# Second feed-forward stage: masks ahead of a store in the queue, another order at its head, and a last tile finished in four blocks of 128 rows

## The chip, the core and the metric

The kernel is one program on one core of a Trainium2 chip. TensorE (PE), VectorE (DVE), ScalarE (ACT) and GpSimd (POOL) compute; SyncE (SP) issues most of the transfers, POOL some of them. Each engine works through its own list of instructions in order and waits on semaphores that the others raise. The metric is the device time of one execution in microseconds (us); the time given is the median of several executions.

## The reference

A macaron block on x of shape (2, 4096, 256), float32: half a feed-forward stage, attention, half a feed-forward stage.

```
x = x + 0.5 * ffn(layernorm(x))
x = x + attention(layernorm(x))
x = x + 0.5 * ffn(layernorm(x))

ffn(x):
    x_mixed = mix_kernel[0] * x[s-1] + mix_kernel[1] * x[s] + mix_kernel[2] * x[s+1]
    h       = x_mixed @ W1[p] + b1[p]             for nine experts p, 64 wide
    paths   = h @ W2[p] + b2[p]
    scores  = tanh(x_mixed @ Wo1 + bo1) @ Wo2 + bo2
    out     = paths[argmax(scores)]               one expert for each row
    return layernorm(x + out) * gamma + beta
```

The attention takes the absolute value of causal scores, a softmax over them, and its values. The expert's choice is a one-hot row, which the kernel multiplies onto the hidden values of all nine experts.

## The kernel before

**Tiles.** The 8192 rows are 16 tiles of 512 rows; a tile lies as 4 blocks of 128 rows beside each other. `ffn(0)` is the first feed-forward stage, `attention(0)` and `attention(1)` follow, and `ffn(1)` is the second stage. The order on every engine is written out by hand. Each stage has a head, in which tiles 0 to 2 are brought under way, and then the turns t = 0 to 16. In one turn the engines work on several tiles at once: the output product of tile t, the hidden values of tile t+1, the choice of tile t+2, the mixed rows of t+3 and the normalisation of t+5.

**The choice and its masks.** ACT takes tanh (`scores`, L1412), PE multiplies with Wo2 (`route`, L1853), and DVE finds the highest of nine scores in five small steps (`choose`, L929 to L942). PE transposes the one-hot rows (`choice`, L1862), ACT writes them out as `oh_t` (`one_hot`, L1424), and SP's `spread` stores `oh_t` to `oh_scratch` (L467), waits until it has landed, and loads it back three times, spread over the partitions as the mask of five chunks (L472, L474, L476).

**The hidden values.** For each of five chunks c PE forms `hidden(t, c)`, six 512-column matmuls (part of L1756), and DVE adds the bias and multiplies with the mask: `masked(t, 0)` is L956 (both inputs from SBUF), the others are L959 (one input from PSUM). ACT rounds pairs of chunks to float16 (`masked_high`, L1432) and DVE takes what is left over (`masked_low`, L965). PE's `path(t, c)` multiplies them with W2, for chunks 0 to 3 in 12 matmuls of 256 columns, three for each block of rows, and for chunk 4 in float32 (L1882, four matmuls, recorded as eight). Within a chunk it goes over the four blocks, so all four are complete only behind the last matmul of the tile.

**The mixed rows.** `mixed_before` (L818) and `mixed_behind` (L826) on DVE add the two neighbours onto what ACT has begun (`middle`, L1377). ACT's `x_high` (L1385) and DVE's `mixed_low` (L833) split the sum into two float16 parts; `hidden(t, 0)` waits for the second. ACT's `normalised` is L1363 and `transposed` L1369; PE's `transposed` is L1764.

**The end of a tile.** `result` (L913, DVE) adds the product onto the tile's rows. ACT squares and sums them (`squares`, L1393), POOL makes the inverse root (`result_scale`, L606 and L610), and DVE scales (`result_scaled`, L849, four instructions of 256 columns with both inputs from SBUF). POOL has meanwhile added beta onto the residual rows (`residual`, L620, 1024 columns) and then issues an accumulating transfer from them onto the result (`residual_added`, L630). SP stores the tile when that has landed (`store`, L486). Only for the program's last tile does DVE add the residual itself (`result_added`, L857).

**Around the second stage's head.** The last attention tile's rows are normalised and added on DVE (`output`, L870 and L872), measured by `output_sums` (L878), and then stored to `x2_scratch` (L524). That store stands in SP's list ahead of the second stage's first `spread`.

## Time and profile before

| | us |
|---|---|
| median of 3 executions | 1434.1 (1433.8 to 1434.25) |
| the profiled execution | 1429.62 |
| its span, first to last instruction | 1427.8 |
| PE busy in it | 1330.3 |
| DVE busy | 1150.4 |
| ACT busy | 923.0 |
| POOL busy | 314.5 |
| mean granted clock of TensorE | 0.985 |

The profiled execution is the one that the views are taken from, and its time is 1.8 us more than its span and 4.5 us less than the median of the others. The granted clock is a share of full speed: 1.00 is 2.4 GHz and 0.50 is 1.2 GHz. A step in a timeline is from one instruction's start to the next one's, which is a little shorter than the duration shown, since instructions of one engine overlap at their ends.

### The profile page before, as it was taken

To read this page: it belongs to the slowest core of one execution; us is meant where nothing else is said; L and a number is where in the kernel's file an instruction comes from. 1 tells how busy PE (TensorE), PEld (TensorE's weight loads), DVE (VectorE), ACT (ScalarE), POOL (GpSimd) and SP (SyncE) were. 2 spreads that over 40 slices of the span, in tenths; PEclk is the share of its full clock that TensorE was granted. 3 is DMA by queue.
4 is the path that set the end of the run, shared out by engine and by line. 5 is a ranking of instruction groups with operands and counts; after the bars stand their busy time and mean duration, and the time that the engine had idled before them with its cause. 6 is when DMAs were issued, how large, how long until landed. Compare 5 with 4: busy or idle time off the path is not lost.

```text
span 1427.8 us, 24659 instructions
## 1 busy us (share of the span) xinstructions
PE 1330.3 (93%) x7700; PEld 769.9 (54%) x7700; DVE 1150.4 (81%) x2295; ACT 923.0 (65%) x1717; POOL 314.5 (22%) x390
## 2 busy tenths in 40 slices
PE   4899999989999999998989999999998869999996
PEld 2577766754445454544444445454544336767764
DVE  7789999887778787778876778787878777888875
ACT  6676776465666766665865666766666876776741
POOL 2254454360101000310030101000310003444433
PEclk8999999999999999999999999999999999999998
DMA  6165554440010000102010010000102212555544
GB/s 178 35 157 141 138 153 123 123 119 0 31 45 16 29 30 0 46 0 90 30 45 1 30 45 16 29 30 1 45 1 91 72 36 60 144 137 140 128 107 118
DMA packets 91449, 98.43 MB, mean 69 GB/s; under 512 B 9035, under 2 KB 87380, under 8 KB 91348
## 3 DMA queue, kind: packets, MB, share of 16 engines
q1 hardware_dynamic: 86884, 80.91, 19.0%
q0 software_dynamic: 4464, 16.25, 6.0%
q8 instruction: 54, 0.88, 0.3%
q14 instruction: 47, 0.39, 0.1%
HBM read 55.43 MB, written 25.46 MB: 57 GB/s over the span
## 4 chain that ended last, share of the span: by engine, by line
PE 72%; DVE 14%; ACT 6%; issue 4%; DMA 0%; DVEq 0%; POOL 0%; ACTq 0%; SPq 0%; POOLq 0%
PE PS L1756 64%; PE PS L1882 3%; DVE R L1164 2%; DVE R L1158 2%; PE PS L1764 2%; DVE run_max L1152 2%; PE PS L1853 2%; ACT R L1596 2%; ACT R L1600 1%; DVE x_st L878 1%; ACT R L1555 1%; DVE R L849 1%; DVE R L959 1%; PE PS L1862 1%; DVE st L783 1%
## 5 line engine op out<-in xcount | busy, mean ns | idle before, releaser
L1756 PE MATMUL PS<-R 128*128 128x512 f16 (+3 forms) x3456 | 722.4, 364 | 37.0 <-DVE R L1164 27.6
L1756 PEld LDWEIGHTS PS<-R 128*128 128x128 f16 (+1 forms) x3456 | 327.5, 98 | 398.6 <-DVE R L1164 54.2
L1164 DVE TENSOR_TENSOR R<-R 128x512 f16<-128x512 f32 (+3 forms) x288 | 188.9, 656 | 99.4 <-ACT R L1600 97.6
L1587 ACT ACTIVATE R<-PS 128x512 f32 (+5 forms) x288 | 160.1, 557 | 160.5 <-PE PS L1756 160.4
L1596 ACT ACTIVATE R<-R 128x512 f32<-128x512 f32 (+4 forms) x288 | 169.6, 589 | 57.3 <-DVE R L1158 56.5
L1756 PE MATMUL PS<-R,w_hi 128*128 128x512 f16 x636 | 193.1, 386 | 9.4 <-DVE R L833 8.6
L1152 DVE TENSOR_TENSOR run_max<-run_max,R 128x512 f32<-128x512 f32 (+3 forms) x272 | 182.7, 672 | 8.4 <-DVE run_max L1152 1.7
L1756 PE MATMUL PS<-w_hi,R 128*128 128x256 f16 x1024 | 187.7, 273 | 1.5 <-DVE R L913 1.5
L1600 ACT ACTIVATE R<-R 128x512 f16<-128x512 f32 (+3 forms) x288 | 171.1, 594 | 26.7 <-ACT R L1596 0.4
L1158 DVE TENSOR_TENSOR R<-R,max_row 128x512 f32<-128x512 f32 (+4 forms) x288 | 187.0, 649 | 0.5 <-ACT max_row L1664 0.5
L1756 PE MATMUL PS<-w_lo,R 128*128 128x256 f16 x512 | 139.6, 273 | 0.0
L587 POOL TENSOR_SCALAR veps<-mv 128x4 f32<-128x4 f32 x48 | 12.2, 254 | 564.7 <-issue 328.8
L959 DVE SCALAR_TENSOR_TENSOR R<-PS,b1c,R 128x512 f32<-128x512 f32 x128 | 93.0, 743 | 41.5 <-PE PS L1756 41.5
L1756 PE MATMUL PS<-R,w_lo 128*128 128x512 f16 x318 | 122.5, 385 | 0.0
L1756 PEld LDWEIGHTS PS<-w_hi,R 128*128 128x128 f16 x1024 | 100.2, 98 | 27.5 <-DVE R L913 3.5
L665 POOL TENSOR_TENSOR R<-R 128x1024 f16<-128x1024 f32 x16 | 36.0, 2262 | 290.6 <-ACT R L1562 286.9
L1756 PEld LDWEIGHTS PS<-R,w_hi 128*128 128x128 f16 x636 | 60.4, 103 | 56.9 <-DVE R L833 9.9
L965 DVE TENSOR_TENSOR R<-R 128x1024 f16<-128x1024 f32 x64 | 78.0, 1219 | 0.0
L620 POOL TENSOR_TENSOR R<-R,beta_b 128x1024 f32<-128x1024 f32 x32 | 75.2, 2350 | 8.0 <-DVE R L956 8.0
L1393 ACT ACTIVATE R<-R 128x256 bf16<-128x256 f32 x128 | 51.6, 404 | 38.8 <-DVE R L913 38.8
L1369 ACT ACTIVATE R<-PS 128x1024 f32<-128x1024 f32 x32 | 32.8, 1024 | 64.8 <-PE PS L1764 64.7
L1363 ACT ACTIVATE R<-R,shift,rstd 128x256 f32<-128x256 f32 x128 | 66.1, 588 | 10.3 <-POOL shift L599 10.2
(129 smaller groups left out, 1687.9 us busy)
## 6 DMA issues: line engine op xcount, KB each, us to landing
R<-x_scratch SPq DMA_DIRECT2D x48, 512.0 KB, 4.3
x_scratch<-R SPq DMA_DIRECT2D x32, 512.0 KB, 3.1
R<-R POOLq DMA_DIRECT2D x31, 512.0 KB, 4.6
R<-oh_scratch SPq DMA_DIRECT2D x32, 320.0 KB
R<-in_L_attn_x SPq DMA_DIRECT2D x16, 512.0 KB, 5.2
R<-oh_scratch SPq DMA_DIRECT2D x32, 256.0 KB
out<-R SPq DMA_DIRECT2D x16, 512.0 KB, 3.1
R<-in_L_ffn_W SPq DMA_DIRECT2D x2, 288.0 KB
```

The lines of the kernel that those rows point to most:

```text
L620: g.tensor_tensor(rows4(x_rows(t)), rows4(x_rows(t)), beta_b[:, :].unsqueeze(1).to_broadcast([P, SUB, D]), ALU.add).then_inc(xb_done, 1)
L959: v.scalar_tensor_tensor(out=at, in0=ps_h[:, h_bank[g, c], :], scalar=b1c[:, c:c + 1], in1=chunk(mask, t, c), op0=ALU.add, op1=ALU.mult).t ...
L965: v.tensor_tensor(chunk(hlo, t, c, n), masked_chunk(t, c, n), chunk(hhi, t, c, n), ALU.subtract)\
L1152: v.tensor_tensor(run_max[:, lo:], run_max[:, lo:], cols(ring, at, TT - lo), ALU.max)\
L1158: v.tensor_tensor(cols(ring, at, TT - lo), cols(ring, at, TT - lo), max_row[:, lo:], ALU.subtract)\
L1164: v.tensor_tensor(p_lo[:, i * TT + lo:(i + 1) * TT], pf[:, (i % 2) * TT + lo:(i % 2 + 1) * TT], p_hi[:, i * TT + lo:(i + 1) * TT], ALU.sub ...
L1363: ins = a.activation(cols(n_rows(t), u * D, D), cols(x_rows(t), u * D, D), ACT.Identity, bias=shift[:, i, u:u + 1], scale=rstd[:, i, u:u + 1])
L1393: ins = a.activation(cols(square, u * D, D), cols(n_rows(t), u * D, D), ACT.Square, accum_out=y_sq[:, u:u + 1])
L1587: a.activation(cols(ring, ring_m + i * TT + lo, TT - lo), ps_s[:, i, lo:], ACT.Abs, scale=1.0 / (QS * XS * D ** 0.5)).then_inc(abs_done, 1)
L1596: a.activation(p, cols(ring, ring_n + i * TT + lo, TT - lo), ACT.Exp)\
L1600: a.activation(p_hi[:, i * TT + lo:(i + 1) * TT], p, ACT.Copy).then_inc(phi_done, 1)
L1756: ins = t_.matmul(dst, w, xx, start=start and n == 0, stop=stop and n == last, skip_group_check=skip)
```

## The change

Six things are different.

1. SP's list: the store of the last attention tile to `x2_scratch` now stands behind the second stage's first `spread`.
2. DVE's list at the head of either stage: `behind(2)` and `mixed_low(2)` are earlier. In the second stage `behind(2)` comes ahead of `choose(1)` too.
3. ACT's list at the head: `x_high(2)` is earlier, and in the second stage `one_hot(1)` comes behind it.
4. POOL's list, in either stage: `residual(15)` moves from turn 15 to turn 14, right behind `residual(14)`, and so ahead of the accumulating transfer of tile 13.
5. PE, second stage, tile 15: `path_by_rows` goes over the blocks of rows outside and the chunks inside, so each block ends with its own float32 matmul. Each block has a PSUM bank of its own (6, 7, 0, 1), and the whole is behind waits for all of the tile's hidden values.
6. The rest of tile 15 is done by block as well: result, squares, inverse root, scaling, adding and store. `residual_added(14)` stands on POOL behind the inverse roots of blocks 0 and 1. The four stores of 128 rows stand in SP's list behind the store of tile 14 and don't wait for one another.

SP's list where attention ends and the second stage begins. L524 is the store to `x2_scratch`, L557 loads the second stage's rows. Before:

```order
164 L524 DMA x_scratch<-R 128x4x256
165 L557 DMA R<-x_scratch 128x4x256 x3
166 L524 DMA x_scratch<-R 128x4x256
167 L467 DMA oh_scratch<-oh_t 9x512
168 L472 DMA R<-oh_scratch 64x5x512
169 L474 DMA R<-oh_scratch 64x4x512
```

And after (L506 is the store to `x2_scratch`, L472 that of `oh_t`, L477 to L481 the mask loads):

```order
165 L571 DMA R<-x_scratch 128x4x256 x3
166 L472 DMA oh_scratch<-oh_t 9x512
167 L477 DMA R<-oh_scratch 64x5x512
168 L479 DMA R<-oh_scratch 64x4x512
169 L481 DMA R<-oh_scratch 9x512
170 L506 DMA x_scratch<-R 128x4x256
```

The store has moved behind the four transfers of tile 0's mask.

DVE's list at the head of the second stage, from `mixed_before` of tile 2 on. Before:

```order
1581 L818 SCALAR_TENSOR_TENSOR R<-R,kmix 128x512 x2
1582 L956 TENSOR_TENSOR R<-R 128x512
1583 L959 SCALAR_TENSOR_TENSOR R<-PS,b1c,R 128x512
1584 L929 TENSOR_REDUCE r_max<-PS 128x4
...
1588 L942 TENSOR_TENSOR oh<-r_pr,r_top 128x36
1589 L959 SCALAR_TENSOR_TENSOR R<-PS,b1c,R 128x512
1590 L826 SCALAR_TENSOR_TENSOR R<-R,kmix 128x512 x2
1591 L959 SCALAR_TENSOR_TENSOR R<-PS,b1c,R 128x512
1592 L965 TENSOR_TENSOR R<-R 128x1024
1593 L959 SCALAR_TENSOR_TENSOR R<-PS,b1c,R 128x512
1594 L833 TENSOR_TENSOR R<-R 128x1024
```

And after (L1013 and L1016 are `masked`, L859 `mixed_behind`, L866 `mixed_low`, L986 to L999 `choose`, L1022 `masked_low`):

```order
1581 L851 SCALAR_TENSOR_TENSOR R<-R,kmix 128x512 x2
1582 L1013 TENSOR_TENSOR R<-R 128x512
1583 L1016 SCALAR_TENSOR_TENSOR R<-PS,b1c,R 128x512
1584 L859 SCALAR_TENSOR_TENSOR R<-R,kmix 128x512 x2
1585 L986 TENSOR_REDUCE r_max<-PS 128x4
...
1589 L999 TENSOR_TENSOR oh<-r_pr,r_top 128x36
1590 L1016 SCALAR_TENSOR_TENSOR R<-PS,b1c,R 128x512 x2
1591 L866 TENSOR_TENSOR R<-R 128x1024
1592 L1022 TENSOR_TENSOR R<-R 128x1024
```

`mixed_behind` stands ahead of the choice, and `mixed_low` ahead of the first `masked_low` and of the mask of chunk 4.

POOL's list at the end of the program. Before:

```order
368 L610 TENSOR_TENSOR y_rstd<-y_var,half 128x4
369 L620 TENSOR_TENSOR R<-R,beta_b 128x1024
370 L630 DMA R<-R 128x1024
371 L606 TENSOR_SCALAR y_var<-y_sq 128x4
372 L610 TENSOR_TENSOR y_rstd<-y_var,half 128x4
373 L620 TENSOR_TENSOR R<-R,beta_b 128x1024
374 L630 DMA R<-R 128x1024
```

And after (L637 is the beta addition, L647 the accumulating transfer, L651 and L654 the inverse root of a block):

```order
367 L627 TENSOR_TENSOR y_rstd<-y_var,half 128x4
368 L637 TENSOR_TENSOR R<-R,beta_b 128x1024 x2
369 L647 DMA R<-R 128x1024
370 L623 TENSOR_SCALAR y_var<-y_sq 128x4
371 L627 TENSOR_TENSOR y_rstd<-y_var,half 128x4
372 L651 TENSOR_SCALAR last_var_s<-y_sq 128x1
373 L654 TENSOR_TENSOR last_rstd_s<-last_var_s,half 128x1
374 L651 TENSOR_SCALAR last_var_s<-y_sq 128x1
375 L654 TENSOR_TENSOR last_rstd_s<-last_var_s,half 128x1
376 L647 DMA R<-R 128x1024
```

The last beta addition has moved up by one turn, and four small instructions stand ahead of the last accumulating transfer.

The diff, cut to its core (the parts on SP's and DVE's lists that the rows above show are left out):

```
...
+                def store_by_rows(t):
+                    for u in range(SUB):
+                        sp.wait_ge(last_added, u + 1)
+                        sp.dma_start(dram_tile(dst, t)[:, u, :],
+                                     cols(n_rows(t), u * D, D)).then_inc(last_stored[u], 16)
...
+                def row_scale(u):
+                    pool.wait_ge(last_sq, u + 1)
+                    g.tensor_scalar(last_var_s[:, u:u + 1], y_sq[:, u:u + 1], 1.0 / D, EPS, ALU.mult, ALU.add)\
+                        .then_inc(last_eps, 1)
+                    pool.wait_ge(last_eps, u + 1)
+                    g.tensor_tensor(last_rstd_s[:, u:u + 1], last_var_s[:, u:u + 1], half[:, u:u + 1], ALU.pow)\
+                        .then_inc(last_rstd, 1)
...
                 def turn(t):
-                    if on(t - 1):
+                    if on(t - 1) and not by_rows(ph, t - 1):
                         result_scale(t - 1)
-                    if on(t):
+                    if on(t) and t < NTT - 1:
                         residual(t)
-                    if on(t - 1) and not by_vector(ph, t - 1) and not left_over(ph, t - 1):
+                    if t == NTT - 2:
+                        residual(NTT - 1)
+                    if by_rows(ph, t):
+                        row_scale(0)
+                        row_scale(1)
+                    if on(t - 1) and not by_rows(ph, t - 1) and not left_over(ph, t - 1):
                         residual_added(t - 1)
+                    if by_rows(ph, t):
+                        row_scale(2)
+                        row_scale(3)
...
+                def last_turns(t):
+                    result(t - 1)
+                    row_result(t, 0)
+                    row_result(t, 1)
+                    result_scaled(ph, t - 1)
+                    row_result(t, 2)
+                    dve.wait_ge(xb_done, use(ph, t) + 1)
+                    row_added(t, 0)
+                    row_added(t, 1)
+                    row_result(t, 3)
+                    row_added(t, 2)
+                    row_added(t, 3)
...
-                one_hot(1)
+                if ph == 0:
+                    one_hot(1)
+                    x_high(ph, 2)
+                else:
+                    x_high(ph, 2)
+                    one_hot(1)
                 masked_high(0, 0)
-                x_high(ph, 2)
                 masked_high(0, 1)
...
+                def path_by_rows(t):
+                    g = use(ph, t)
+                    pe.wait_ge(nT_done, g + 1)
+                    pe.wait_ge(hlo_done, groups_before(ph, t) + len(GROUPS) - 1)
+                    pe.wait_ge(hm_done, HC * g + HC)
+                    for u in range(SUB):
+                        dst = PS[:, ROW_BANKS[u], 0:D]
+                        for c in range(LAST):
+                            split_product(dst, [((cols(chunk(hhi, t, c), u * P, P), cols(chunk(hlo, t, c), u * P, P)),
+                                                 (w2_hi[:, c, :], w2_lo[:, c, :]))],
+                                          c == 0, False, skip=True)
+                        t_.matmul(dst, cols(masked_chunk(t, LAST), u * P, P), w2_last[:, :], start=False, stop=True,
+                                  skip_group_check=True).then_inc(last_psum, 1)
...
```

`row_result`, `row_added` and `row_squares` are the block's share of `result`, of `result_scaled` with the addition behind it, and of `squares`.

## Rows read from the trace of the kernel before

**Rows 1.** The page: busy time, granted clock by fortieths, chain's shares by engine

```profile
PE 1330.3 (93%) x7700; PEld 769.9 (54%) x7700; DVE 1150.4 (81%) x2295; ACT 923.0 (65%) x1717; POOL 314.5 (22%) x390
...
PEclk8999999999999999999999999999999999999998
...
PE 72%; DVE 14%; ACT 6%; issue 4%; DMA 0%; DVEq 0%; POOL 0%; ACTq 0%; SPq 0%; POOLq 0%
```

**Rows 2.** Chain of waits, second stage's head: start us, length us, what

```profile
1162.56 0.38 SPq L524
...
1163.04 2.63 DMA oh_scratch<-oh_t
...
1167.06 3.90 DMA R<-oh_scratch
...
1170.98 0.69 DVE R L956
...
1178.98 1.48 PE PS L1756 x6
```

**Rows 3.** Timelines there: start us, us, engine, line, operation, xcount, [idle before <-releaser]

```profile
1156.26 0.59 ACT L1424 ACTIVATE oh_t<-PS 9x512 f16<-9x512 f16 x1
...
1168.18 2.08 ACT L1363 ACTIVATE R<-R,shift,rstd 128x256 f32<-128x256 f32 x4
...
1164.78 1.41 DVE L818 SCALAR_TENSOR_TENSOR R<-R,kmix 128x512 f32<-128x512 f32 x2 [0.85 <-ACT R L1377]
...
1167.69 0.38 PE L1756 MATMUL PS<-R,w_lo 128*128 128x512 f16 x1
...
1174.44 0.27 SPq L467 DMA_DIRECT2D oh_scratch<-oh_t  x1
1175.81 0.58 SPq L472 DMA_DIRECT2D R<-oh_scratch  x1
```

**Rows 4.** Windows: length, busy PE, PEld, DVE, ACT, POOL, granted clock, DMA

```profile
47.00:49.00 2.00, 1.79 (x5) 0.70 (x6) 2.00 (x5) 0.00 (x0) 0.00 (x0) 0.53 0.09 16
...
1163.00:1165.00 2.00, 1.01 (x3) 0.43 (x4) 1.15 (x2) 1.91 (x3) 0.00 (x0) 0.57 0.77 255
...
1174.00:1178.00 4.00, 2.07 (x14) 1.29 (x12) 4.00 (x7) 4.00 (x5) 0.00 (x0) 1.00 0.11 37
```

**Rows 5.** Chain of waits, first stage's head

```profile
45.94 1.23 DVE R L833
...
47.21 2.76 PE PS L1756 x6
...
50.81 1.03 PE PS L1853 x8
```

**Rows 6.** Timelines of POOL and DVE, second stage, turns 14 to 16

```profile
1400.07 2.33 POOL L620 TENSOR_TENSOR R<-R,beta_b 128x1024 f32<-128x1024 f32 x1
...
1403.09 1.22 DVE L965 TENSOR_TENSOR R<-R 128x1024 f16<-128x1024 f32 x1
1405.10 0.75 DVE L959 SCALAR_TENSOR_TENSOR R<-PS,b1c,R 128x512 f32<-128x512 f32 x1 [0.79 <-PE PS L1756]
...
1412.87 3.76 DVE L849 SCALAR_TENSOR_TENSOR R<-R,y_rstd,gamma_b 128x256 f32<-128x256 f32 x4 [3.17 <-POOL y_rstd L610]
...
1420.94 1.67 DVE L849 SCALAR_TENSOR_TENSOR R<-R,y_rstd,gamma_b 128x256 f32<-128x256 f32 x4 [3.17 <-POOL y_rstd L610]
```

**Rows 7.** Timelines of POOL, PE and SP at the program's end

```profile
1411.80 1.03 POOL L610 TENSOR_TENSOR y_rstd<-y_var,half 128x4 f32<-128x4 f32 x1
...
1416.93 0.92 POOL L630 DMA_DIRECT2D R<-R  x1 [1.77 <-DVE R L849]
...
1413.10 1.89 PE L1882 MATMUL PS<-w_last,R 128*128 128x256 f32 x8
...
1421.51 0.37 SPq L486 DMA_DIRECT2D out<-R  x1
...
1424.48 0.37 SPq L486 DMA_DIRECT2D out<-R  x1
```

73 lines of the change are left out of this document (52 added, 21 removed).

## The prediction

> **What bounds the kernel now.** The page comes first [rows 1]: PE is busy for 93% of the span at full clock nearly everywhere, and the chain of waits stands on PE for 72% of it. In the middle of each stage PE runs without a gap, so what DVE, ACT or SP do there costs nothing. Time can be had only where PE waits: at the heads of the two feed-forward stages and behind PE's last matmul. The change touches these three places, and one place where PE was not waiting.
>
> I then followed the chain through the second stage's head [rows 2]. The reader is to see that it leaves the compute engines: it goes through the store of the last attention tile, the store of the one-hot rows (2.63 us until landed) and the mask loads (3.90 us behind the last issue), and DVE's first masking starts at 1170.98, when they have landed. From there it stays on DVE until `mixed_low(2)` ends, and PE's `hidden(2, 0)` starts at 1178.98. Behind that nothing but PE's own work is on the chain, so what 1178.98 moves by, the rest of the program moves by. The one-hot rows had been ready since 1156.85 (1156.26 and 0.59 in [rows 3]). SP could not take them up before 1163.04, because the store ahead of them waited for DVE's sums until 1162.56.
>
> **Second stage's head, the queue.** With the order of SP changed, the one-hot store is issued at about 1156.9. In the next turn the mask loads follow it by 1.37 us (1174.44 to 1175.81 in [rows 3]); here it was 2.7 us, with the 512 KB store in front. So the loads are issued from 1158.2 to 1159.6, and with the 3.90 us of [rows 2] they have landed by 1163.5. That is ahead of any use: DVE ends `mixed_before(2)` at 1166.1, its start being set by ACT (1164.78, 1.41 in [rows 3]). The displaced store waits for the same sums and still goes out at 1162.56.
>
> **Second stage's head, what is late next.** I walk the new list of DVE with the durations of before. `masked(0, 0)` runs at 1166.1. `masked(0, 1)` needs PE's `hidden(0, 1)`, whose last matmul ends at 1168.07 (1167.69, 0.38 in [rows 3]), so it starts at 1168.2. Without the idle time between, `mixed_behind(2)` follows at 1168.8 and the choice at 1170.2. Two maskings take 1171.2 to 1172.5, and `mixed_low(2)` 1172.5 to 1173.7; ACT's rounding in front of it is done by 1171.3, because `normalised(4)` ends at 1170.25 (1168.18, 2.08 in [rows 3]) and about 1 us of `x_high` follows. PE reaches `hidden(2, 0)` behind the choice, `hidden(0, 4)` and the transposes at 1173.8, the same moment. So it starts at 1173.8 for 1178.98: **5.2 us** less. Followed on, ACT's `normalised(5)` will wait about a microsecond for POOL, because DVE's list as a whole ends less early than `hidden(2, 0)`; ACT has longer idle time than that behind it, ahead of its next one-hot copy, which covers it. Tile 1's mask moves up with its one-hot rows and is not late. Bounds: 4.2 us, if the mask loads or a semaphore cost a little more, and 5.8 us, if the half-clock stretch at 1163 [rows 4] shrinks too.
>
> **First stage's head.** Here the masks are in time, and the chain runs over DVE to `mixed_low(2)` at 45.94 and PE at 47.21 [rows 5]. DVE's work has the same length in either order, but `mixed_behind(2)` moves ahead of both first maskings and `mixed_low(2)` right behind them, past four instructions of 3.1 us together (two maskings, `masked_low(0, 0)`, the masking of chunk 4), so to 42.8. PE then has `hidden(0, 4)` 1.3 us later than before, since the mask of chunk 1 frees its bank behind `mixed_behind(2)`, and comes to `hidden(2, 0)` at 45.1. The six matmuls took 2.76 us here, against 1.48 us in the second stage [rows 2, 5], at a granted clock of 0.53 [rows 4], behind the wait for `mixed_low(2)`. That wait is gone, with a shorter one, for the bank, in its place. At full clock the scores are ready at 46.6, ACT takes them up at 47.3, when it has its rounding behind it, and the router's matmuls start at 48.1 for 50.81: **2.7 us** less. At half clock it would be 2.1 us. I take full clock, because PE was busy for only 2.07 us of 4.00 from 1174 to 1178 and the clock stayed at 1.00 [rows 4]. DVE and ACT gain less than PE at first, since the length of DVE's list sets them; both stand idle in the following turn for longer than the difference, so PE does not wait for it.
>
> **The moved beta addition.** `residual(15)` now starts when `residual(14)` ends, at 1402.4 in the times of before, and runs for 2.3 us [rows 6]. Beside it stand a masking from PSUM and, from 1403.09, `masked_low(15, 0)`. The trace shows what an operation of DVE with both inputs from SBUF pays beside such an addition: `result_scaled` took 3.76 us at 1412.87 and 1.67 us at 1420.94 [rows 6], so 2.1 us for 2.3 us of overlap. The overlap is 1.7 us now, the price 1.5 us, and the masking behind it has 0.79 us of idle time in front (1405.10 in [rows 6]). So 0.7 us come through to DVE's later work. In the second stage this is part of the tail's sum below. In the first stage the same two operations meet; there PE works on tile 15 while `masked_low(15, 1)` is done and takes up a part, so I charge **0.5 us** (bounds 0 and 0.8).
>
> The Trainium skill, in "SBUF — State Buffer", section "Who interferes with whom", says that a DVE instruction with two SBUF inputs and a GpSimd instruction that reads SBUF share a port pair, and that the later one blocks fully. By that rule `masked_low(15, 0)` would start only at 1404.7 and each of the two charges would be 0.2 us more; the trace's 3.76 us agree with it within 0.2 us, and it is the rule that speaks against this part of the change.
>
> **The tail.** A 256-column matmul is 0.11 us, half of what one of the six of 1.48 us takes once their overlap is off [rows 2]. Tile 15's 48 of them ended where the float32 ones begin, at 1413.10 [rows 7], so they had begun at 1407.9, without a wait. Now PE waits for the second `masked_low(15)`, which ends at 1409.2 (the masking at 1405.10 and 0.65 us later, 0.66 us of step, 1.6 us of `result_scaled(13)`, 1.2 us of its own). A block is 12 of the matmuls and a quarter of the float32 stretch of 1.89 us [rows 7], less its overlap: 1.75 us together. So the blocks are complete at 1411.1, 1412.9, 1414.6 and 1416.4, where all of it was at 1415.0. DVE ends the result of tile 14 at 1410.3, ACT's squares and POOL's root follow, and the root is ready at 1413.45, for 1412.83 (1411.80, 1.03 in [rows 7]). `result_scaled(14)` then runs without the beta addition beside it and ends at 1415.1, where it ended at 1416.63. POOL issues the accumulating transfer when this is done and the roots of blocks 0 and 1 are behind it. A root of four columns is 1.03 us; of one column none stands in the trace. I take 0.6 us, between 0.2 and 1.55 us (the longest, beside DVE), and so the issue at 1415.4, for 1416.93 [rows 7]. Tile 14's store followed it by 4.58 us (1421.51 in [rows 7]), so it goes at 1420.0. By then DVE has the last block added (1420.0), and four stores follow at 0.4 us each, the last at 1421.6. Before, the last store waited for tile 14's to land and went at 1424.48 [rows 7], 2.9 us before it had landed. Now 1 MB is in the queues at once: 2.9 us for the first half, some 1.6 us more for the second, or 1424.6. That is **2.8 us** less. Bounds: 1.0 us, with roots of 1.5 us and the transfer at 1417.2; 3.5 us, with short roots and small stores that land sooner.
>
> **The sum** is 5.2 + 2.7 - 0.5 + 2.8 = 10.2 us. The profiled execution would be 1429.6 - 10.2 = 1419.4 us, and with the median's distance of 4.5 us kept, 1434.1 - 10.2 = **1423.9 us**. The bounds add up to 6.5 us (4.2 + 2.1 - 0.8 + 1.0) and 12.1 us (5.8 + 2.8 - 0 + 3.5).
>
> **Rivals.**
>
> *The tail gives only 1 us.* The last accumulating transfer is still ahead of everything in SP's queue, and now has two roots in front of it on POOL. With 1.3 us and more for a root and its variance, it is issued no earlier than before, and only the stores that no longer wait for one another are left. Sum 8.4 us, 1425.7 us. For it: a root has fixed work that fewer columns may not shorten. Against: the old list had 2.3 us of beta addition in the same place on POOL, and that is gone.
>
> *The mask was not alone.* At the second head some other wait ends late, for instance the loads land later, or PE falls to half clock at 1171 to 1178. Each stretch of six matmuls then costs 1.3 us more [rows 2, 5]; with two such, 7.6 us remain, 1426.5 us. Against it: DVE is the only engine between the mask and `hidden(2, 0)`.
>
> *Gains swallowed.* If the 1.4 us that PE now stands idle at 1407.9 put it at half clock for tile 15, its 7 us of matmuls grow to 14, and the sum is about 3 us: 1431 us, at the edge of what a measurement can tell.
>
> *Slower.* One mechanism: TensorE's clock stays at its lower level after the second head. At half clock each microsecond of matmuls costs another one. So 10.2 us of matmuls at half clock that had full clock before bring the time back to 1434.1 us, and from there on the change is slower; at 13 us it is 0.2% slower, 1437 us. For it only that the clock does fall there, 0.57 at 1163 [rows 4]; against it that it was back at 1.00 by 1174, although PE was less busy then than it will be.
>
> **How the numbers follow.** Forecast 64% (own range 1422.4 to 1425.0), short tail 17% (1425.7), second head short 9% (1426.5), swallowed 6% (1431), slower 4% (1437). To hold eight in ten the range takes the upper bound of the gain, the short tail and part of the second head: 1421.8 to 1427.6. A measurement of this kernel can tell about 0.2%, 2.9 us, from no change. All of the first three cases are beyond that; of the swallowed one I count half as no change. Faster 0.92, same 0.04, slower 0.04.
>
> **What the profile afterwards would show.** In the second head the one-hot store at about 1154.7 (1156.9 less the 2.2 us of the first stage), ahead of the 512 KB store; no idle time of DVE on a transfer; `hidden(2, 0)` 9.0 us behind the start of `mixed_before(2)`, where it was 14.2 us (1164.78 to 1178.98). In the first head the router's matmuls of tile 2 at 48.1. At turn 14 a `masked_low` of about 2.7 us. At the end four stores within 1.7 us behind that of tile 14, and the accumulating transfer issued 1.5 us earlier than before against PE's first matmul of tile 14. Wrong would be the forecast if DVE still waits for `oh_scratch`, if PE's clock shows 0.5 beyond the places named, or if the last accumulating transfer is not issued before SP's blocks are ready.

## The result, and the profile after

| | before | after |
|---|---|---|
| median of 4 executions | 1434.17 us (1433.8 to 1435.5) | 1419.71 us (1418.93 to 1421.44) |
| the profiled execution | 1429.62 us | 1418.93 us |
| its span | 1427.8 us | 1417.1 us |
| mean granted clock | 0.985 | 0.988 |

The ratio of the medians is 0.9902 (95% interval 0.989 to 0.9914): 14.5 us less. The forecast was 1423.9 us, with a range from 1421.8 to 1427.6. The direction was right, the gain was about 4 us larger than forecast, and the time lies below the range.

The two profiled executions differ by only 10.7 us, half a microsecond from the predicted sum of 10.2 us. The terms of that sum were not right one by one, though, and the other 3.8 us are the distance between a profiled execution and the median: 4.5 us for before, 0.8 us for after. Both points lead to the same cause, TensorE's clock.

The page of after, the lines that answer to [rows 1]:

```profile
PE 1329.5 (94%) x7700; PEld 770.8 (54%) x7700; DVE 1152.0 (81%) x2301; ACT 925.2 (65%) x1717; POOL 326.9 (23%) x396
...
PEclk9999999999999999999999999999999999999999
...
PE 73%; DVE 15%; ACT 7%; issue 4%; POOL 0%; DMA 0%; DVEq 0%; ACTq 0%; POOLq 0%; SPq 0%
```

PE's busy time is 0.8 us less, so nearly all of the 10.7 us is, on balance, PE's idle time. Half-clock stretches that went and others that came nearly cancel in the busy time, as the places below show.

**The second head.** SP's timeline of after (start, length, what), where [rows 2] had the store to `x2_scratch` at 1162.56 ahead of the one-hot store:

```profile
1152.45 0.31 SPq L472 DMA_DIRECT2D oh_scratch<-oh_t  x1
1153.84 0.60 SPq L477 DMA_DIRECT2D R<-oh_scratch  x1
...
1158.13 0.41 SPq L506 DMA_DIRECT2D x_scratch<-R  x1
```

And DVE's, from `mixed_before(2)` on. `masked(0, 0)` (L1013) now starts without a wait:

```profile
1160.42 1.41 DVE L851 SCALAR_TENSOR_TENSOR R<-R,kmix 128x512 f32<-128x512 f32 x2 [0.92 <-ACT R L1434]
1161.75 0.68 DVE L1013 TENSOR_TENSOR R<-R 128x512 f32<-128x512 f32 x1
1164.90 0.75 DVE L1016 SCALAR_TENSOR_TENSOR R<-PS,b1c,R 128x512 f32<-128x512 f32 x1 [2.46 <-PE PS L1827]
```

The mask is no longer what is late. DVE's new idle time, 2.46 us, is ended by PE, and the chain of waits shows why (start, length, what):

```profile
1159.56 5.30 PE PS L1827 x12
1164.86 0.85 PE PS L1924 x8
...
1170.91 1.31 PE PS L1827 x6
```

The twelve matmuls of `hidden(1, 0)` and `hidden(0, 1)` take 5.30 us. `hidden(2, 0)`, at 1178.98 in [rows 2], starts at 1170.91; 4.4 us of that were won ahead of this head. It follows the start of `mixed_before(2)` in 10.49 us, where 9.0 was predicted. PE had run dry before that, and the windows (columns as in [rows 4]) give the clock:

```profile
1155.00:1157.00 2.00, 0.00 (x0) 0.00 (x0) 1.62 (x3) 2.00 (x5) 0.00 (x0) 1.00 0.63 180
1157.00:1159.00 2.00, 1.36 (x8) 0.96 (x8) 1.82 (x5) 1.49 (x3) 0.00 (x0) 0.76 0.47 120
1159.00:1161.00 2.00, 1.44 (x4) 0.58 (x5) 1.08 (x2) 2.00 (x3) 0.00 (x0) 0.50 0.78 262
```

The granted clock is 0.50, the lower of its two levels (1.2 GHz), up to 1164.9.

**The first head.** The chain of after, where [rows 5] had `hidden(2, 0)` at 47.21 and the router at 50.81:

```profile
41.94 2.74 PE PS L1827 x6
...
45.91 1.31 PE PS L1827 x6
...
48.07 1.03 PE PS L1924 x8
49.10 5.22 PE PS L1827 x36
```

The six at 41.94 are `hidden(0, 4)`, 2.74 us at half clock behind a wait of 2.17 us for the bank. `hidden(2, 0)` itself ran at full clock.

**The end.** `masked_low(15, 0)` on DVE and the two beta additions on POOL at turn 14, for [rows 6]:

```profile
1391.84 4.66 POOL L637 TENSOR_TENSOR R<-R,beta_b 128x1024 f32<-128x1024 f32 x2
...
1394.85 2.73 DVE L1022 TENSOR_TENSOR R<-R 128x1024 f16<-128x1024 f32 x1
```

The second addition ran from 1394.15 to 1396.50. PE's last tile, POOL's roots and SP's stores, for [rows 7]:

```profile
1401.07 0.27 PE L1827 MATMUL PS<-w_hi,R 128*128 128x256 f16 x1 [1.28 <-issue]
...
1402.37 0.60 PE L1973 MATMUL PS<-w_last,R 128*128 128x256 f32 x2
...
1404.12 0.60 PE L1973 MATMUL PS<-w_last,R 128*128 128x256 f32 x2
...
1405.33 0.49 POOL L651 TENSOR_SCALAR last_var_s<-y_sq 128x1 f32<-128x1 f32 x1
1405.89 0.67 POOL L654 TENSOR_TENSOR last_rstd_s<-last_var_s,half 128x1 f32<-128x1 f32 x1
1406.65 0.35 POOL L651 TENSOR_SCALAR last_var_s<-y_sq 128x1 f32<-128x1 f32 x1
1407.08 0.55 POOL L654 TENSOR_TENSOR last_rstd_s<-last_var_s,half 128x1 f32<-128x1 f32 x1
1407.59 0.92 POOL L647 DMA_DIRECT2D R<-R  x1
...
1412.58 2.48 SPq L493 DMA_DIRECT2D out<-R  x4
```

Blocks end 1.75 us apart, at full clock.

**A place that the change does not touch.** The second batch of the attention begins at about 750. Before PE's long run there it waits for DVE twice. The timeline of PE, before:

```profile
748.95 1.46 PE L1756 MATMUL PS<-R 128*128 128x512 f16 x6 [2.60 <-DVE R L1135]
751.67 4.88 PE L1756 MATMUL PS<-R 128*128 128x512 f16 x11 [1.27 <-DVE R L1164]
```

And after:

```profile
747.05 1.46 PE L1827 MATMUL PS<-R 128*128 128x512 f16 x6 [2.60 <-DVE R L1192]
749.78 2.55 PE L1827 MATMUL PS<-R 128*128 128x512 f16 x11 [1.27 <-DVE R L1221]
```

The same instructions, the same two waits to the hundredth, and 4.88 us against 2.55 us for the same eleven matmuls. The chain's row there, before and then after:

```profile
751.67 9.98 PE PS L1756 x42
...
749.78 7.32 PE PS L1827 x42
```

That is **2.66 us** less, and no term of the prediction was for it.

**Where the 10.7 us are.** DVE starts the same 48 reductions in every kernel (the router's maximum and the maximum of an attention tile). The differences of their starts cut the span into stretches. Each number of this table is the gain of that kernel's trace in that stretch against the first trace of before, in us; a minus is a loss. A column's time is that of the reduction in the first trace of before that ends the stretch.

| trace | up to 39 | first head, to 68 | to 740 | to 762 | to 1155 | second head, to 1198 | to 1383 | to the end |
|---|---|---|---|---|---|---|---|---|
| after | 1.03 | 1.71 | -0.85 | 2.66 | -0.12 | 3.81 | 0.00 | 2.46 |
| after_again | 0.08 | 1.67 | -0.84 | 2.67 | 0.02 | 3.65 | 0.00 | 2.47 |
| before_again | 1.04 | -2.74 | 0.15 | 0.03 | 0.01 | 0.00 | -0.01 | -0.02 |
| masks_first | 0.64 | 0.00 | 0.38 | 0.15 | 0.01 | 0.92 | 0.00 | -0.01 |
| first_head | 0.04 | 1.67 | -0.54 | 2.66 | 0.01 | -2.89 | 0.00 | 0.01 |
| second_head | 0.70 | -2.84 | 0.10 | 0.02 | -0.01 | 5.11 | 0.00 | 0.01 |
| orders | 0.05 | 1.67 | 0.89 | 2.09 | -0.02 | -0.06 | -0.01 | -0.01 |
| heads | 0.98 | 1.70 | -0.45 | 2.66 | 0.00 | 3.56 | -0.01 | 0.00 |
| tail | 1.28 | -2.73 | -0.19 | 0.21 | 0.01 | -2.88 | 0.00 | 2.45 |
| shifted | 0.30 | 1.68 | -1.26 | 0.15 | 0.03 | -2.95 | 0.00 | -0.01 |
| warm | 2.67 | -0.20 | -0.61 | 2.66 | 0.06 | 6.41 | 0.00 | 2.48 |
| beta_early | -0.38 | 1.67 | 0.77 | 2.03 | 0.06 | 4.40 | -0.71 | 3.72 |
| warm_early | 2.99 | -0.20 | -0.08 | 2.66 | 0.05 | 6.41 | -0.71 | 3.72 |

The sum of the row of after is 10.7 us. The columns up to 39 and to 740 scatter by about a microsecond and more between kernels that have the same instructions there (before_again, the same kernel, has 1.04 us up to 39), so little is read from them: one difference of 0.58 us, and the filler's effect on the first, both below. The others take few values again and again. How it comes to these is what the experiments are about.

### The profile page after: what moved, and what is told of

The parts are those of the page before. It is cut to its first block, busy times and chain, and to the rows that moved or that the text cites. A ratio compares the mean times of both kernels' runs of the same rounds, so it can differ in the third digit from the quotient of the medians.

```text
span 1417.1 us, 24674 instructions
## 1 busy us (share of the span) xinstructions
PE 1329.5 (94%) x7700; PEld 770.8 (54%) x7700; DVE 1152.0 (81%) x2301; ACT 925.2 (65%) x1717; POOL 326.9 (23%) x396
## 4 chain that ended last, share of the span: by engine, by line
PE 73%; DVE 15%; ACT 7%; issue 4%; POOL 0%; DMA 0%; DVEq 0%; ACTq 0%; POOLq 0%; SPq 0%
PE PS L1827 64%; PE PS L1953 3%; PE PS L1835 3%; DVE R L1221 2%; DVE R L1215 2%; DVE run_max L1209 2%; PE PS L1924 2%; ACT R L1667 2%; ACT R L1671 1%; DVE x_st L905 1%; ACT R L1626 1%; DVE R L1016 1%; DVE st L816 1%; DVE R L1022 1%; PE PS L1933 1%
## 5 line engine op out<-in xcount | busy, mean ns | idle before, releaser
L1016 DVE SCALAR_TENSOR_TENSOR R<-PS,b1c,R 128x512 f32<-128x512 f32 x128 | 92.9, 743 | 42.5 <-PE PS L1827 42.5
L1022 DVE TENSOR_TENSOR R<-R 128x1024 f16<-128x1024 f32 x64 | 81.1, 1267 | 0.0
L637 POOL TENSOR_TENSOR R<-R,beta_b 128x1024 f32<-128x1024 f32 x32 | 75.1, 2349 | 3.2 <-DVE R L1013 3.2
L1835 PE MATMUL PS<-ident,R 128*128 128x128 f32 x384 | 55.5, 288 | 18.6 <-ACT R L1420 15.8
```

Of the source, the lines that this page charges most:

```text
L637: g.tensor_tensor(rows4(x_rows(t)), rows4(x_rows(t)), beta_b[:, :].unsqueeze(1).to_broadcast([P, SUB, D]), ALU.add).then_inc(xb_done, 1)
L1016: v.scalar_tensor_tensor(out=at, in0=ps_h[:, h_bank[g, c], :], scalar=b1c[:, c:c + 1], in1=chunk(mask, t, c), op0=ALU.add, op1=ALU.mult).t ...
L1022: v.tensor_tensor(chunk(hlo, t, c, n), masked_chunk(t, c, n), chunk(hhi, t, c, n), ALU.subtract)\
L1835: ins = t_.transpose(dst[:, u * P:(u + 1) * P], cols(rows, u * D + c * P, P), ident[:, :])
```

## The experiments

The first two groups ran on one chip, the third on another; each group has its own median of before: 1432.08, 1431.49 and 1431.33 us. Ratios are to that, with their 95% intervals.

### First group: the parts by themselves

**The kernel before once more**, for a second trace and as a measure of the noise.

> The kernel before, unchanged, profiled a second time. Theory A (executions of one program differ by stretches in which TensorE is granted half its clock, at places where it had stood idle): the times spread over some 4 us around 1434 us, and the new trace, compared step by step with the first one, differs only in such stretches, each worth 1 to 3 us, at the first stage's head, where attention goes over to the second batch (750 us), and at the second stage's head. Theory B (the 4.5 us between the first profiled execution and the median are a fixed cost outside the program, which the change happens to remove): the span of this execution is again about 1428 us and the time stays 4.5 us above it or more.

Measured 1431.7 us, ratio 1.0000 (0.9991 to 1.0009). The profiled execution took 1431.14 us, again 1.8 us more than its span, so theory B's fixed cost outside the span is not there. Its trace was longer than the first by 1.5 us, and the first head lost 2.74 us in it. Its chain:

```profile
46.17 2.76 PE PS L1756 x6
...
49.77 1.84 PE PS L1853 x8
51.62 7.16 PE PS L1756 x36
```

Of the same 36 matmuls after has 5.22 us, and 1.03 us for the router's eight. The first trace of before had full clock here (1.03 us for the eight in [rows 5]). So one kernel can have, or lack, a further stretch at half clock behind the same work, and the trace from which I predicted was one that lacked it. Of the four further traces with the old first head three have it (before_again, second_head, tail: 2.73 to 2.84 us); of those with the new order and no filler in the head none has. Against before as three of its five traces have it, the first head thus gains 4.4 us (1.67 and 2.74).

**Only SP's order.** The store of the last attention tile behind the one-hot rows, all else as before.

```diff
+                    if ph == 1 and t == -ROUTE:
+                        last = B * NT - 1
+                        sp.wait_ge(x2_sums, SUB * last + SUB)
+                        sp.dma_start(dram_tile(x2_t, last), rows4(xr)).then_inc(x2_stored, 16)
...
-                store(NT - 1)
+                else:
+                    store(NT - 1)
```

> The kernel before with one thing changed: the last attention tile's store stands behind the second stage's first mask transfers in SP's list. DVE's and ACT's orders and the tail are those of before. Theory A: DVE no longer waits for the mask loads, and walking its old list gives hidden(2, 0) 2.6 us earlier, so 1431.5 us; with a longer half-clock stretch at that head 1.3 us less of it, 1433 us. Rival (the queue was all of it, the orders add nothing): 5 us, 1429 us.

Measured 1429.92 us, ratio 0.999 (0.9979 to 1.0001), single executions from 1425.8 to 1433.4: 2.2 us under the group's before, which the interval does not tell from nothing. In the trace the wait for the mask is gone, and `hidden(2, 0)` gains only 0.92 us, where theory A had 2.6 us or, with a longer half-clock stretch, 1.3 us. DVE's timeline:

```profile
1164.94 0.68 DVE L961 TENSOR_TENSOR R<-R 128x512 f32<-128x512 f32 x1
1168.15 0.75 DVE L964 SCALAR_TENSOR_TENSOR R<-PS,b1c,R 128x512 f32<-128x512 f32 x1 [2.53 <-PE PS L1761]
```

`masked(0, 0)` comes 6 us earlier than at 1170.98 (1.2 us of it won ahead of this head), PE's `hidden(0, 1)` is the next thing late, and behind it the old list still puts `mixed_low(2)` last. The clock was low here too: the twelve matmuls ahead of that masking took 5.30 us. The queue alone is not enough.

**Both heads, the old end**: parts 1 to 3 of the change, that is the edit above, ACT's part 3, and in DVE's list of either stage:

```diff
+                    behind(2)
...
+                    mixed_low(ph, 2)
...
-                    behind(2)
...
-                    mixed_low(ph, 2)
```

> The kernel before with both heads changed (SP's queue, and DVE's and ACT's orders in both stages), and the old tail. Theory A: 3.8 to 5.2 us at the second head and 1.7 to 2.7 us at the first, so 1426.2 to 1428.7 us, the lower end only where the clock does not fall. Rival (the heads are worth more than the profile shows, because idle time of TensorE is what brings its clock down): 9 us or more, under 1425 us, with fewer half-clock stretches than before in the trace.

Measured 1421.15 us (1420.78 to 1421.37), ratio 0.9923 (0.9909 to 0.9936): 10.9 us less without the new end. Theory A had 5.5 to 7.9 us, the rival 9 us or more, so the time speaks for the rival. In the trace the heads themselves have 1.70 and 3.56 us; 2.66 us more are at the second batch's start, which the edit does not touch.

**Only the end**: parts 4 to 6 of the change, with the old heads.

```diff
+                    if t == NTT - 2:
+                        residual(NTT - 1)
+                    if by_rows(ph, t):
+                        row_scale(0)
+                        row_scale(1)
```

> The kernel before with the tail changed (last tile by blocks, residual(15) moved to turn 14 in both stages), and the old heads. Theory A: 2.5 us at the end less 0.5 us in the first stage, 1432.1 us. Rival (the blocks are worth more than their stretch of the trace shows, outside the span or in the executions without a profile): 5 us or more, 1429 us or less.

Measured 1431.94 us, ratio 0.9997 (0.9988 to 1.0006). That is the 1432.1 us expected, but by luck: 2.0 us less than 1434.1 had been meant, and it is 0.1 us less than the group's own before. By the time alone this part would seem to be worth nothing. By the trace it gives 2.45 us at the end, as in after. In the same trace the old second head lost 2.88 us. A window there, with the clock in the last column but two:

```profile
1184.00:1188.00 4.00, 4.00 (x15) 2.10 (x15) 3.23 (x10) 2.84 (x6) 0.00 (x0) 0.50 0.01 4
```

In the trace of before_again the same 1184 to 1188 had 29 matmuls, and a clock of 1.00. The second head stands more than 200 us ahead of the part that was changed, so this loss is not its doing through any wait; the one change ahead of it is the moved beta addition in the first stage.

### Second group: head by head

**The change once more**, with the group's own before.

> The changed kernel again, beside the parts below on one chip. The heads alone took 10.9 us off the kernel before, where their stretches of the trace promised 6 to 8; the tail alone took nothing. Theory A (the tail is worth 2.5 us less the 0.5 us of the moved addition whatever stands before it, and was hidden in its own run by a longer half-clock stretch at the second head): 2.0 us under the heads alone, a gain of 12.9 us, 1419.2 us. Rival (the tail is worth nothing in a median): a gain of 11 us, 1421 us.

Measured 1420.24 us (1419.87 to 1421.07), ratio 0.992 (0.9907 to 0.9934), 11.2 us less. The kernel after has the same median within 0.5 us in both comparisons; it is before that had 1434.17 us in the first comparison and 1431.3 to 1432.1 us in the groups. The gain is that of the heads alone and 0.3 us, where theory A had 2.0 us for the end; the rival, that the end is worth nothing in a median, comes closer. The traces show the 2.47 us at the end, and against that of heads 0.90 us less up to 39 and 0.6 us for the moved addition in the first stage. Across the groups after is 0.9 to 1.4 us below heads. So the end's 2.5 us less 0.6 us are shown in the traces, of which the medians show 0.3 to 1.4 us.

**Only the first head.** DVE's and ACT's new order in the first stage.

```diff
@@ DVE, first stage
+                    behind(2)
                     masked(0, 0)
...
+                    mixed_low(ph, 2)
```

> The kernel before with DVE's and ACT's new orders in the first stage's head alone. In the two traces with the new first head TensorE kept its full clock behind that head (from 48 us on) and where attention goes over to the second batch (748 to 756 us); in the four traces without it the clock fell there. Theory C (the first head decides both, the one because the long wait is gone, the other because everything behind is moved by 2 us): the trace shows full clock at both places, and the median gains 2.7 + 1.9 + 2.5 us, 6 to 7 us, 1425.5 us. Rival D (each place falls or not by itself, and the second one did not by chance): 2.7 to 4.5 us, 1428.5 us, with half clock at 750 us in the trace.

Measured 1428.26 us, ratio 0.9973 (0.9962 to 0.9984). The trace has the 1.67 us at the head and the 2.66 us at the second batch's start, and then loses 2.89 us at the second head, whose code is that of before. So the clock did at the first two places what theory C said, and the time is that of rival D (1428.5 us). The eight matmuls of the router and the 36 behind them in this trace:

```profile
1177.58 1.88 PE PS L1858 x8
1179.46 7.11 PE PS L1761 x36
```

It is the loss that the tail had, in the same place.

**Only the second head.** SP's new order and DVE's and ACT's in the second stage.

```diff
@@ DVE, second stage
                     masked(0, 1)
+                    behind(2)
                     choose(1)
...
+                    mixed_low(ph, 2)
                     masked_low(0, 0)
```

> The kernel before with the second stage's head alone changed (SP's queue, and DVE's and ACT's orders there). Theory C: the half-clock stretches of the first head and of the second batch's start stay, and the gain is what the second head's stretch of the trace shows, 3.8 to 4.5 us, 1428 us. Rival (the second head carries the unexpected part): 6 us or more, 1426 us or less.

Measured 1426.77 us, ratio 0.9963 (0.9949 to 0.9976): 4.7 us less, a little more than theory C's 3.8 to 4.5 us. In the trace it is 5.11 us, where 5.2 had been predicted for it. Its chain:

```profile
1166.02 4.07 PE PS L1766 x12
...
1176.08 1.31 PE PS L1766 x6
```

`mixed_before(2)` starts at 1166.81 here, so `hidden(2, 0)` follows in 9.27 us; 9.0 us was predicted. The twelve matmuls that took 5.30 us in after take 4.07 us.

**The new orders with the old queue.** DVE's and ACT's lists in both stages as in after, SP's as before; against after this takes away:

```diff
-                    if ph == 1 and t == -ROUTE:
-                        last = B * NT - 1
-                        sp.wait_ge(x2_sums, SUB * last + SUB)
-                        sp.dma_start(dram_tile(x2_t, last), rows4(xr)).then_inc(x2_stored, 16)
```

> The kernel before with DVE's and ACT's new orders at both heads, but the old queue of SP, so that the second stage's first mask is as late as before. Walking DVE's new list from 1170.98 gives hidden(2, 0) 1.8 us earlier at the second head. Theory C: that beside all of the first head's 6 to 7 us, 8 to 9 us together, 1423.5 us. Rival D: 4.5 to 6.3 us, 1427 us.

Measured 1424.75 us, ratio 0.9948 (0.9934 to 0.9962), 6.7 us less, which lies between rival D and theory C. At the second head the trace has -0.06 us, for an expected 1.8. DVE's timeline has the old wait again:

```profile
1166.70 0.69 DVE L956 TENSOR_TENSOR R<-R 128x512 f32<-128x512 f32 x1 [4.51 <-DMA R<-oh_scratch]
```

So in the traces the queue alone gives 0.92 us, the orders alone nothing, both together 5.11 us. Part of this is the clock again. In masks_first the twelve matmuls and the router's eight behind them took 6.47 us, in second_head 4.86 us. In orders PE waited 3.05 us for the choice, and the matmuls behind that ran at half clock: 0.59 us for 0.32 us (the choice's four) and 2.62 us for 1.40 us (the next six). At second_head's clock, an estimate from these lengths, the queue alone would give 2.5 us and the orders alone about 1.4 us, 3.9 us together for 5.11. The parts belong together, but most of the contrast is the clock.

### Third group: the clock itself

**The first head and 1.75 us of filler.** As first_head, with eight more 512-column matmuls ahead of the transposes of tile 13, in the middle of the first stage, whose product nobody reads. It asks whether the second batch's start hangs on the order at the head or on the moment at which the work comes by.

```diff
+                if g == 13:
+                    for _ in range(8):
+                        t_.matmul(ps_n[:, 0, :], ident16[:, :], w1_hi[:, 0, 0:TT], start=True, stop=True)
```

> The kernel with the first stage's new orders alone, and eight extra 512-column matmuls on TensorE in the middle of that stage (tile 13, into a bank that is overwritten; the result doesn't change), which move all that follows by 1.75 us. In five of five traces with the new first head TensorE kept its full clock where attention goes over to the second batch, in five of five without it the clock fell there, at a price of 2.7 us. Theory C (what decides is by how much everything there is moved): moved back by 1.75 us, the clock falls at 750 us again, and the time is 1.75 + 2.7 us above the first head alone, 1432.7 us. Rival E (the new first head itself leaves the clock in a better state): full clock at 750 us, 1.75 us above, 1430 us.

Measured 1430.2 us (1429.14 to 1431.68), ratio 0.9995 (0.9986 to 1.0004). The first head keeps its 1.68 us. The second batch's start gives 0.15 us in place of 2.66. The windows there:

```profile
748.00:752.00 4.00, 2.81 (x9) 0.95 (x10) 3.85 (x10) 2.85 (x6) 0.00 (x0) 0.66 0.00 0
752.00:756.00 4.00, 4.00 (x10) 1.36 (x9) 2.15 (x8) 0.83 (x2) 0.00 (x0) 0.50 0.01 4
```

First_head has 1.00 in both. So the new order alone does not secure the 2.66 us: in this trace, with 1.75 us of work 550 us earlier, they are gone, though nothing that PE waits for at 750 is different: the six and the eleven matmuls start 2.73 us apart in first_head and in shifted (747.77 and 750.50, 748.22 and 750.95). Only, in shifted the six take 1.76 us for 1.46, so the clock fell while they ran. This holds for the one execution that was traced, and at 1431.68 us it was the longest of eleven. The median of 1430.2 us is rival E's 1430 and not theory C's 1432.7, and it is 1.9 us above first_head's, about what the filler itself costs. So it is not shown that the shift takes the gain away as a rule.

**Filler in PE's waits at the heads.** The change, with PE computing 23 products in the first head and 17 in the second that nobody reads (one group of 4 stands in both), where it would have waited; the 13 first of the second head stand behind the wait for the last attention tile.

```diff
                     route(0)
+                    filler(4)
                     choice(0)
+                    filler(6)
...
+                    pe.wait_ge(x2_done, SUB * NTT)
+                    filler(13)
                 transposed(ph, 3)
+                filler(4)
...
+                if ph == 0:
+                    filler(9)
```

> The changed kernel with extra 512-column matmuls (identity by weights, into a bank that is overwritten) where TensorE waits in the two heads: 4 and 6 around the first choice, 9 behind the second one, 13 and 4 around the transposes of tile 3 in the second head. Theory A (half clock follows idle time): both heads run at full clock; the second head gains the 2.6 us that its 12 matmuls lost, the first 1.4 us behind the second choice and up to 1.5 us from 28 us on: 4 to 5.5 us under the changed kernel, 1415.5 us. Rival (the stretches do not follow the idle time, or the extra matmuls delay the waiting ones): no gain, 1420 us or more.

Measured 1416.43 us (1415.02 to 1418.02), ratio 0.9895 (0.9878 to 0.9912). The second head gives 6.41 us. Its chain and a window:

```profile
1159.41 2.76 PE PS L1827 x12
...
1168.17 1.31 PE PS L1827 x6
```

```profile
1156.00:1160.00 4.00, 3.56 (x20) 1.81 (x19) 3.18 (x6) 3.67 (x6) 0.00 (x0) 1.00 0.66 192
```

The twelve matmuls are at 2.76 us, and the clock stays at 1.00 through the head. This closes the account of the second head. From the start of the twelve to the end of the router's eight behind them it is 4.86 us in second_head, 6.15 in after, 3.56 in warm, and the gains are 5.11, 3.81 and 6.41 us. In all seven traces with the new second head (also after_again, heads, beta_early and warm_early) the sum of this time and the gain is 9.96 or 9.97 us. So what the head gained differs by the time at half clock alone.

In the first head it is not shown that the filler gave anything. The clock was at 1.00 from 28 to 48 us, where after has 0.53 and 0.62 from 28 to 36 and 0.73 and 0.84 from 40 to 48, and then fell behind it:

```profile
48.00:52.00 4.00, 4.00 (x19) 2.49 (x18) 3.84 (x15) 0.59 (x1) 2.87 (x3) 0.60 0.00 0
```

Its gain up to 39 us (2.67) and its loss behind (-0.20) add up to 2.5 us, in warm_early to 2.8 us; in the seven traces with the new first head and no filler there the sum goes from 1.3 to 2.7 us. The half-clock time became shorter, but what is left of it falls where PE works without a gap. As a whole warm is 3.3 to 3.8 us below the medians of after, where 4 to 5.5 us had been expected. PE's timeline shows the fall in the midst of work, 2 us behind the end of a wait of 1.77 us, where the same kind of matmul goes from 0.38 to 0.45 us and the ones of 256 columns take 0.42 us for 0.27:

```profile
46.67 1.03 PE L1924 MATMUL PS<-wo,th 65*128 65x9 f32 x8 [1.77 <-ACT th L1477]
...
47.98 0.38 PE L1827 MATMUL PS<-R,w_lo 128*128 128x512 f16 x1
...
48.63 0.45 PE L1827 MATMUL PS<-R,w_lo 128*128 128x512 f16 x1
48.87 0.42 PE L1827 MATMUL PS<-w_hi,R 128*128 128x256 f16 x1
```

**The beta addition two turns earlier.** The change, with `residual(15)` at turn 12.

```diff
-                    if t == NTT - 2:
+                    if t == NTT - 4:
```

> The changed kernel with the last beta addition of either stage (residual(15)) another two turns earlier, at turn 12, where DVE has idle time. Theory A (beside that addition masked_low(15, 0) took 2.73 us for 1.22 us, and that set back tile 15 on TensorE in both stages): masked_low(15, 0) is back at 1.22 us, the first stage gains 0.5 us and the tail 0.7 us, 1.2 us together, 1419 us. Rival (the collision goes to another instruction that TensorE waits for): no gain.

Measured 1418.48 us (1417.6 to 1419.05), ratio 0.9909 (0.9893 to 0.9924). Theory A's 1419 us is met and so is the rival's sign: `masked_low(15, 0)` takes 1.21 us again, and the instruction that pays is `mixed_low` of another tile, L866:

```profile
1363.90 4.67 POOL L637 TENSOR_TENSOR R<-R,beta_b 128x1024 f32<-128x1024 f32 x2
...
1367.11 2.55 DVE L866 TENSOR_TENSOR R<-R 128x1024 f16<-128x1024 f32 x1
...
1394.63 1.21 DVE L1022 TENSOR_TENSOR R<-R 128x1024 f16<-128x1024 f32 x1
```

The end gives 3.72 us for 2.46, but 0.71 us are lost in the stretch just ahead, where that `mixed_low` stands. In the first stage the 0.58 to 0.60 us that every kernel with the addition at turn 14 loses between 256 and 311 us are gone (0.01 us). By the traces the move is worth 1.1 us; by the times, whose intervals overlap those of after, it can't be told from nothing.

**Both.** The filler and the earlier addition.

```diff
-                    if t == NTT - 2:
+                    if t == NTT - 4:
...
+                    filler(13)
```

> Both of these edits in one. Theory A: 5 to 6.5 us under the changed kernel, 1414.5 us, the fastest of all. Rival: with other starting times the clock falls at a place where it did not before, such as the second batch's start, and 2 to 3 us of that are lost again.

Measured 1415.84 us (1414.75 to 1417.27), ratio 0.9893 (0.9878 to 0.9909), 15.5 us less than its before, for 1414.5 us expected. The clock did not fall at the second batch's start (2.66 us gained there). Its median is the lowest of all, 0.6 us under warm's, which the spread of either does not separate. All executions of it and of warm are below the lowest of after (1418.93 us), though after was timed in other groups.

## Why the prediction was right or wrong

**The second head's queue and order: right.** The one-hot store went at 1152.45, which is 1156.9 less the 4.4 us that the program was ahead there; no wait of DVE for a transfer is left; the 512 KB store follows the mask loads and hurts nobody. The term of 5.2 us was for the clock of the trace of before, and in second_head it measured 5.11. The other six traces with this head have from 3.56 to 6.41 us, so that the number was met in one of them is a matter of its clock. The experiments also bear out that neither the queue nor the order does all of it alone, which the walk through DVE's list had implied.

**Its size in the changed kernel: wrong by 1.4 us.** The step that failed is the bound that the half-clock stretch at 1163 might only shrink. In after it is longer: 5.30 us for the twelve matmuls, against 3.92 in before. That was the rival "the mask was not alone" by its price of 1.3 us for each six matmuls, in another place than the one that I named: ahead of 1165, not from 1171 to 1178. With the router's eight behind them counted in, after_again and heads lost a little more, and had 3.65 and 3.56 us.

**The first head: the time was right, the reasons were not.** The router was predicted at 48.1 and came at 48.07. But 1.03 us of that were won ahead of 39 us, in work that the change does not touch and where unchanged kernels scatter by as much. The head itself gave 1.7 us. The step that failed is the choice of full clock: I took it because a wait was gone, though the same paragraph names the new, shorter wait, for the bank. That one ended in `hidden(0, 4)` at half clock, 2.74 us. The alternative in the text, 2.1 us, was nearer.

**The moved beta addition: right.** `masked_low(15, 0)` took 2.73 us for 2.7 predicted, and 2.70 us at 276.23 in the first stage. Each kernel with the addition at turn 14 has just these two, and no kernel without it has one. The charge of 0.5 us in the first stage measured 0.58 us. The rule in the Trainium skill, "SBUF — State Buffer", section "Who interferes with whom", that the later of the two blocks fully, would have the instruction end 1.22 us behind the addition's end at 1396.50, at 1397.72. It ended at 1397.58, so the trace agrees within 0.14 us.

**The end: right in kind, 0.3 us short.** 2.46 us for 2.8. PE waited 1.28 us ahead of tile 15 (1.4 predicted), the blocks were 1.75 us apart (1.75), a root of one column took 0.55 to 0.73 us (0.6). Its variance, which I had not costed beside it, took 0.29 to 0.49 us where the one of four columns took 0.19. The 1.55 us that the prediction calls the longest root of four columns is the usual one beside DVE's work; the longest in that trace took 2.23 us. `result_scaled(14)` was done, and the transfer waited behind the root of block 1 until 1407.59: against `result(13)` it was issued 1.10 us earlier than before, not 1.5. The four row stores were issued in 2.48 us, 0.6 us each and not 0.4. In the medians less than this has arrived (see the second run of the change).

**"The median's distance of 4.5 us kept": wrong, by 3.8 us.** This step, one clause of the sum, cost the range. It treats the profiled execution's distance to the median as a constant of the program. What the traces show in its place is half-clock stretches that one execution has and another has not, 2.74 us of the distance by one of them alone; the rest is not traced. The first trace of before had no such stretch behind its first head, which cost 2.74 us in three of the four others with that head. With it that trace would have been 1432.4 us, in the middle of before's times in the three groups (1429.05 to 1434.03, the second run of before included). The recorded clocks agree with this: the twelve executions above 1433 us have a mean clock of 0.980 to 0.982, the ten below 1430 us 0.984 to 0.987. After never had the stretch in its two traces, and its trace and its median are 0.8 us apart. I had the means to see this: a profiled execution 4.5 us below three others that agree within 0.5 us is a trace of something unusual. The range should have gone down by that distance. Two small slips stand beside it: 1434.1 less the upper bound of 12.1 is 1422.0 and not 1421.8, and the chances as listed give 0.93 for faster and 0.03 for the same.

**The sum: 10.7 us for 10.2, by luck.** The second head, the first head and the end were 1.4, 1.0 and 0.3 us short, and the stretches from 68 to 740 and from 762 to 1155 lost 1.0 us, where 0.5 had been charged. What made up for it, 2.66 us at the second batch's start and 1.03 us up to 39, had no term.

**What had no term: the second batch's start, 2.66 us.** I read the 72% of the chain on PE as time that only less work could shorten, and looked for half-clock stretches only where the change was. The trace of before showed this one too: the windows from 748 to 760 have 0.78, 0.50 and 0.86. It has others, in places that the change does not touch: 0.50 from 28 to 36, 0.64 from 318 to 326, 0.72 from 674 to 680. The same is in after (0.57 from 318 to 326). So one of the prediction's own signs of being wrong, a clock of 0.5 beyond the places named, was there, and the trace of before already had it.

**The other rivals.** PE's clock did not fall behind the new wait ahead of tile 15, so the gains were not swallowed there. The clock did not stay down behind the second head in after; but the rival "slower" named a mechanism that is real. In first_head, tail and shifted 2.9 us were lost at the old second head in just that way, though never 10.

**What stays open.** Why before had 1434.17 us in the first comparison and 1431.3 to 1432.1 in the others, while after moved by 0.5 us: no trace of an execution of that length was taken. A plausible cause is one more stretch of 2 to 3 us at the old second head, as the three traces had it; that is argued, not shown; the low clocks of the executions above 1433 us fit it. And what decides at 750: in eight traces with the new first head the gain is 2.03 to 2.67 us (in the two lowest, orders and beta_early, the clock had fallen too: 0.72 and 0.63 from 748 to 752, and 1.00 behind that), in the five with the old one 0.0 to 0.2 us, and in shifted, which has the new one and 1.75 us more of work, 0.15 us. The moment by the trace's own zero nearly sorts them: all that gained came by 0.9 us or more ahead of before, all that did not at most 1.0 us. Only one pair is the wrong way round, by 0.1 us: masks_first, 1.0 us ahead, gained nothing, and after_again, 0.9 us ahead, gained 2.67. So the moment stays a candidate, and so does something that runs apart from the program. One trace for each kernel does not settle it.

## What to carry to other kernels

A TensorE wait can cost twice: once as a wait, and again as matmuls at half clock, whose place and length differ between executions and can differ with an edit far ahead of them. List every stretch of the trace with a granted clock below 1 before pricing an edit, the ones far from it too, and give the range the sum of these as they stand and as they could be. Where the profiled execution is further from the others than they are among themselves, that distance belongs into the range and not into the forecast; and where two edits feed one wait, price them together, since the parts alone need not add up to the whole.

## What the runs showed of the hardware

- The same eleven matmuls behind the same two waits (2.60 and 1.27 us) took 4.88 us in one kernel and 2.55 us in the other. What PE has just done does not by itself tell the clock that it will get. The fall can also come behind the wait, in the midst of work: at 48.6 us in warm, 2 us after PE had resumed.
- Gains and losses by clock come in few sizes in these traces: 2.03 to 2.67 us at the second batch's start, 2.73 to 2.84 us behind the first head, 2.88 to 2.95 us at the old second head.
- Filler matmuls in PE's waits held the clock at 1.00 through a head that otherwise fell to 0.50 (2.76 us for 5.30 us of matmuls), and in another head took away two stretches at half clock (from 28 and from 42 us) and got one at 48.8 us, where PE had no gap.
- Single columns are not cheap on GpSimd: 0.55 to 0.73 us for a root of 128x1, and 0.29 to 0.49 us for the multiply-add ahead of it, with DVE at work beside them. With 128x4 before took 1.03 and 0.19 us at its end, and mostly 1.55 and 0.52 us in mid-stage beside DVE.
